# A 64-expert layer that sorts three of four batches instead of two, with its gathers and part of the next attention moved across the layer boundary

## The chip, the cores and the metric

The kernel runs on one core of a Trainium2 chip. The metric is device time in microseconds (us) of one execution, lower is better; times of several executions are given by their median.

## The reference, cut to what matters

The kernel is a decoder of four layers of three blocks on x of 4 batches x 512 tokens x 128 features, all in float32. The change touches the last block of layer 2 (64 experts), the first block of layer 3 (causal attention with 16 heads of 8 features), and, by a few lines, the gated delta rule (first block of layer 2).

```python
def _L2_ffn_ref(hidden_states, gate_w, w_gate, w_up, w_down):      # TOP_K = 8, 64 experts, D = 128, F = 96
    scores = softmax(x @ gate_w.T)
    topk_w, topk_ids = top_k(scores, TOP_K)
    topk_w = topk_w / (topk_w.sum(-1) + 1e-20)
    # every token through its 8 experts: silu(x @ w_gate[e].T) * (x @ w_up[e].T) @ w_down[e].T, weighted sum

def _L3_attn_ref(x, ...):                                          # H = 16, head size 8
    att = where(causal, q @ k.T / sqrt(8), -inf); att = softmax(att)
    y = (att @ v) @ Wo + bo
    return layernorm(y) * gamma + beta

x = x + _L2_ffn_ref(layernorm(x)); x = x + _L3_attn_ref(layernorm(x))
```

## The kernel before, in words

Activations x, y and a lie in SBUF with the 128 features on the partitions and the 4 x 512 tokens along the columns; a batch is 512 columns. Each engine has its own in-order instruction list, and semaphores join them. "Batch" below counts in the order of work where nothing else is said.

`layer8` (L1837) is the 64-expert block. It treats the four batches in two ways.

- Dense: batches 2 and 3 go through all 64 experts, with the weight zero where an expert was not chosen. The work is cut into 96 units (`unit`; two batches x J = 48 blocks of 128 rows of the 64 x 96 hidden features). A unit is three matmuls for the gate and three for the up part on values split in a high and a low half (`three`, L829), then silu on ScalarE (L2174), `scale` (L2324, times the routing weight) and `hidden` (L2330) on VectorE, and one float32 matmul `down` (L2049) that sums up in PSUM. The halves of the weights are made for each block by GpSimd for the first six blocks (L1939, L1941) and by ScalarE and VectorE after that (`split_high` L2169, `split_low` L2334), in three slots.
- Sorted: for batches 0 and 1 VectorE finds for each token its 8 experts and a row number in a list sorted by expert, padded to full tiles of 128 rows (`locate`, `situate`, `code`, `put`; indices are cast at L2305). GpSimd stores each token row eight times in DRAM with indirect DMAs (L1972, 64 of 128 rows each). TensorE then runs the tile stage: 127 tiles, two to a step (`PAIRS` = 64): transposed rows (L2055), gate and up (L2067), a transpose (L2075), down (L2082); VectorE evicts each pair (L2365), SP stores it, and `weigh` (L2293, L2294) sums one of the eight shares at every fourth step. GpSimd gathers the result rows with 64 indirect DMAs (L1979), VectorE multiplies and adds them (`mix`), and TensorE turns them back (`join`, L2088).

The order is routing, 48 dense units (`WIDE_SPLIT` = 24 blocks) with the indirect stores beside them, the tile stage, the other 48 dense units with the gathers and `mix` beside them, join. A store or gather waits for `down` as well, so that at most three are issued to two units.

`causal_attention` (L3072) follows. Its head centres and normalises all batches (L3152 to L3326) and projects q, k and v (L3171, L3173, L3178). A softmax needs each row's maximum first: a "read" (`look`, L3202, with a bfloat16 mask matmul L3198 where it lies on the diagonal) makes 1024 columns of scores, and VectorE takes their maxima (`most`, L3405). There are 20 reads to a batch. The head holds the 20 reads of batch 0 and 4 of batch 1. `turn_most` (L3211) and `shift` (L3414) put the maxima into the queries. Then come 16 units to a batch: `weigh` (L3221) makes transposed scores in two halves, ScalarE takes exponents (L3375), GpSimd's select zeroes what is above the diagonal (L3144), and `values` (L3236) sums up three units later (LAG = 3); four exponent buffers rotate (KEEP = 4). The reads of the next batch are spread over the units, at most two in one. Reads and weights share three pairs of PSUM banks in a ring: an item waits until the item three places ahead of it was consumed. The last part of each batch is the division by the row sums and the projection (`shift_sums` L3245, `project_out` L3249).

The delta rule's units also transpose their keys (L2631, phase KT) and copy them (L2902, phase K_COPY) for the update of the state.

## Time and profile before

| | us |
|---|---|
| median of three runs | 1896.92 (1888.32 to 1905.2) |
| the profiled execution's own time | 1892.54 |
| its span, first to last instruction | 1890.8 |
| expert block, from its first matmul to the attention's first | 1164.9 to 1527.4 |
| attention, head | 1527.4 to 1579.5 |
| attention, units | 1579.5 to 1767.5 |
| mean granted clock of TensorE, share of 2.4 GHz | 0.946 |

Over the whole span TensorE is busy for 89%, VectorE for 60%, ScalarE for 52% and GpSimd for 37%. Such shares are means over stages with different limits; the stages are read one by one below. In a timeline row the first number is the start in us from the span's start, the second the time covered, then engine, line, operation, output and input with their shapes, and in brackets how long the engine was idle before and what it waited for.

### The profile page before, as it was taken

Reading aid. Unit: us, or ns where it says so; the run is one execution under the profiler, and the core shown is the slowest. Engines: PE = TensorE matmul, PEld = TensorE weight load, DVE = VectorE, ACT = ScalarE, POOL = GpSimd, SP = SyncE. Lnnn points to the kernel's source line nnn. Section 1 sums busy time; section 2 is a strip of 40 time slices with the busy share of each in tenths; the row PEclk is TensorE's granted clock in tenths of the full one; section 3 lists DMA queues with packets and bytes.
Section 4 is the critical chain, followed back from the end, with each engine's and each line's share of the span. In section 5 each row is a group of like instructions: output and inputs, shape, how many; then the busy total and the mean of one; then the engine's idle time right before and its main releaser. Section 6 shows DMA issues by size and latency. Waiting matters only on the chain. (4 is left out here: it accounts for less than half of the span.)

```text
span 1890.8 us, 50187 instructions
## 1 busy us (share of the span) xinstructions
PE 1677.6 (89%) x19970; PEld 1202.2 (64%) x19970; DVE 1131.9 (60%) x2410; ACT 977.4 (52%) x2317; POOL 706.1 (37%) x947
## 2 busy tenths in 40 slices
PE   7883899775799999999999878899999999999885
PEld 4332899343457889989888753567996655454332
DVE  5534445559556777877776434676657866555334
ACT  4651444548586666666674435234553253445562
POOL 1103311305256777666775201473006621223101
PEclk9996999886699999999999989899999999999998
DMA  7401786000031000000000040523643200000100
GB/s 298 177 1 57 210 241 204 25 1 1 1 145 48 26 15 25 14 15 25 15 24 16 26 201 1 129 78 110 169 135 83 66 5 1 2 2 1 41 1 24
DMA packets 75929, 125.69 MB, mean 66 GB/s; under 512 B 10728, under 2 KB 55152, under 8 KB 74320
## 3 DMA queue, kind: packets, MB, share of 16 engines
q1 hardware_dynamic: 67696, 106.69, 17.5%
q0 software_dynamic: 6912, 15.61, 2.8%
q8 instruction: 165, 2.70, 0.6%
q14 instruction: 68, 0.56, 0.1%
q10 hardware_dynamic: 1088, 0.13, 0.0%
HBM read 83.73 MB, written 38.67 MB: 65 GB/s over the span
## 5 line engine op out<-in xcount | busy, mean ns | idle before, releaser
L2947 DVE SCALAR_TENSOR_TENSOR big<-bank,pack,big 128x256 f32<-128x256 f32 (+2 forms) x384 | 181.4, 474 | 40.6 <-ACT mask L2836 25.4
L2174 ACT ACTIVATE pack<-bank 128x512 f32<-128x512 f32 x96 | 57.5, 600 | 159.6 <-PE bank L834 93.8
L2643 PE MATMUL bank<-y,pack 128*128 128x262 f32 (+1 forms) x384 | 134.5, 435 | 5.5 <-DVE big L2947 5.1
L3375 ACT ACTIVATE pt<-bank 128x1024 f32<-128x1024 f32 (+3 forms) x128 | 84.2, 704 | 105.7 <-PE bank L3221 105.5
L3405 DVE TENSOR_REDUCE part<-bank 128x8 f32<-128x1024 f32 (+1 forms) x80 | 95.6, 1220 | 68.2 <-PE bank L3202 68.2
L2553 POOL TENSOR_TENSOR big<-big,mask 128x256 f32<-128x256 f32 (+1 forms) x128 | 93.7, 732 | 111.2 <-DVE big L2947 110.0
L2835 ACT ACTIVATE big<-bank,pack 128x256 f32<-128x256 f32 x192 | 91.1, 475 | 84.3 <-PE bank L2643 78.8
L1979 POOL DMA_INDIRECT pack<-results,where x64 | 67.0, 1047 | 151.2 <-PE bank L2049 137.6
L832 PE MATMUL bank<-yh,wl 128*128 128x512 f32 x192 | 113.3, 590 | 10.9 <-DVE a L2330 8.3
L2630 PEld LDWEIGHTS bank<-big 128*128 128x128 f32 x896 | 113.3, 193 | 7.1 <-issue 1.4
L2630 PE MATMUL bank<-big 128*128 128x128 f32 x896 | 116.2, 277 | 0.0
L3144 POOL TENSOR_SCALAR_AFFINE_SELECT pt<-pt 128x256 f32<-128x256 f32 x128 | 54.1, 427 | 156.8 <-ACT pt L3375 156.4
L1203 DVE SCALAR_TENSOR_TENSOR a<-bank,big,a 128x128 f32<-128x128 f32 x184 | 52.0, 344 | 82.4 <-ACT a L1115 72.3
L2049 PE MATMUL bank<-a,big 128*128 128x512 f32 x192 | 98.8, 598 | 0.8 <-DVE a L2330 0.8
L2324 DVE TENSOR_TENSOR pack<-pack 128x512 f32<-128x512 f32 x90 | 62.3, 693 | 50.0 <-ACT pack L2174 30.8
L3202 PE MATMUL bank<-big 32*128 32x128 f32 (+1 forms) x1024 | 84.1, 308 | 1.2 <-DVE part L3405 0.9
L1115 ACT ACTIVATE a<-bank,big 128x128 f32<-128x128 f32 x184 | 52.6, 368 | 59.0 <-PE bank L1012 51.9
L3202 PEld LDWEIGHTS bank<-big 32*128 32x128 f32 x1024 | 66.1, 186 | 24.0 <-issue 15.1
L3221 PE MATMUL bank<-big 32*128 32x128 f32 (+3 forms) x512 | 73.7, 477 | 5.2 <-DVE big L3414 2.5
L1972 POOL DMA_INDIRECT wide_sorted<-y,where x64 | 67.3, 1052 | 25.7 <-issue 17.2
L834 PE MATMUL bank<-yh,wh 128*128 128x512 f32 x192 | 76.3, 398 | 0.0
L833 PE MATMUL bank<-yl,wh 128*128 128x512 f32 x192 | 76.0, 396 | 0.0
(672 smaller groups left out, 4396.7 us busy)
## 6 DMA issues: line engine op xcount, KB each, us to landing
big<-in_experts SPq DMA_DIRECT2D x46, 516.0 KB
big<-in_big SPq DMA_DIRECT2D x1, 9216.0 KB, 25.9
gate<-big SPq DMA_DIRECT2D x32, 256.0 KB
z<-gate SPq DMA_DIRECT2D x16, 512.0 KB
pack<-routing SPq DMA_DIRECT2D x60, 128.0 KB
wide_sorted<-big SPq DMA_DIRECT2D x5, 1472.0 KB, 13.1
pack<-in_pack SPq DMA_DIRECT2D x1, 5910.5 KB, 21.5
pack<-wide_sorted SPq DMA_DIRECT2D x16, 256.0 KB, 3.2
```

The costliest lines, as they stand in the source:

```text
L832: nc.tensor.matmul(out, pl, dh[:, cur], start=start, stop=False)
L833: nc.tensor.matmul(out, ph, dl[:, cur], start=False, stop=False)
L834: return nc.tensor.matmul(out, ph, dh[:, cur], start=False, stop=stop)
L2049: nc.tensor.matmul(sums(n), down_block(n // 2), h(n), start=n < 2, stop=n >= N - 2).then_inc(s["down"], 1)
L2553: nc.gpsimd.tensor_tensor(d, d, tap_of(i)[:, :, c:], ALU.add).then_inc(s["whole"], 1)
L2630: mm4 = lambda out, gr, left_, right: [nc.tensor.matmul(out[:, sl(h % GH, P)], left_(h), right(h), start=True, stop=True) for h in hs(gr)][-1]
L2643: nc.tensor.matmul(haloed(i)[:, :, 3 - halo:], k.w["L2_attn_qkv_w"][:, sl(m, P)], tokens, start=True, stop=True).then_inc(s["raw"], 1)
L2835: nc.scalar.activation(dst3(i), conv_in(i, 0), ACT.Copy, scale=weight(i, 3))
L2947: ins = nc.vector.scalar_tensor_tensor(out=d, in0=conv_in(i, back), scalar=weight(i, 3 - back), in1=d, op0=ALU.mult, op1=ALU.add)
L3202: mm = nc.tensor.matmul(dst[:, gl * S + c * w:][:, 0:w], qj[b][rows, j * S + i * P:][:, 0:P], kd[b][rows, key:key + w], start=kind != 0, s ...
L3375: nc.scalar.activation(dst, src, ACT.Exp, scale=-1.0).then_inc(s["weights"], 1)
L3405: nc.vector.tensor_reduce(dst, src, AX.X, ALU.max).then_inc(s["most"], 1)
```

## The change

- Batches are taken in the order 2, 3, 0, 1. Only batch 2 stays dense: 48 units, one for each block, all before the tile stage; each block's weights are now split for one unit instead of two. `WIDE_POOLED` goes from 6 to 3.
- Batches 3, 0 and 1 are sorted: 96 indirect stores, 159 tiles in 80 pairs, vectors of the routing on 768 columns instead of 512. The stores no longer wait for `down`; they follow the indices directly.
- Between the dense units and the tile stage the first attention batch (batch 2) is centred and normalised, its q, k and v are projected, its own keys are made, and 6 of its 20 reads are taken.
- The gathers and sums move into the attention. GpSimd issues 32 of the 96 gathers at its start, ahead of the first select; the other 64 stand between the selects, one, two or four to a unit. ScalarE scales the gathered rows by their shares (`scale_rows`, 8 activations of 128x128 to a token tile, 96 in all), VectorE sums them with one reduction to a token tile (12 in all), and TensorE turns them back (`join`).
- The attention's head holds the other 14 reads of its first batch. Join, centring, variance, projections and own keys of batch b+1 stand in units 5 to 11 of batch b. Its 20 reads are packed in the last seven units (first batch: 2, 3, 3, 3, 3, 4, 2) or the last five (4, 4, 4, 5, 3).
- Constants are set by VectorE instead of GpSimd; the result rows' semaphores live across both blocks.
- In the delta rule the transposes and copies of the keys are left out in the last four units, whose state is not used again.

```diff
-WIDE_TILES = (2 * S * 8 + 64 * (P - 1)) // P
-WIDE_SPLIT, WIDE_POOLED, WIDE_MAP_AT = 24, 6, 13
-WIDE_MIX_AT = [2 * WIDE_SPLIT + 8 + 16 * i // 3 for i in range(8)]
+K8, WIDE_ORDER = 8, (2, 3, 0, 1)
+WIDE_ROWS = 3 * TB
+WIDE_TILES = (WIDE_ROWS * P * K8 + 64 * (P - 1)) // P
+WIDE_POOLED, WIDE_MAP_AT = 3, 13
...
+        late.qj = [big(24, 4)] + [big(4 * b, 4) for b in range(B - 1)]
+        late.kd = [big(28)] + [big(12 + b) for b in range(B - 1)]
...
+        late.kj = [big(30, 4), big(18, 4)]
...
+        layer8(nc, k, x, y, a, late)
+        causal_attention(nc, k, x, y, a, late)
...
-            for m in range(3, WIDE_POOLED):
-                split(m)
             pool.wait_ge(k.wide_cleared, 16 * -(-WIDE_TILES // SORTED))
-            pool.wait_ge(s["rows_ready"], 2)
+            pool.wait_ge(s["rows_ready"], 3)
             pool.wait_ge(s["placed"], 1)
-            for i in range(HALF):
+            for i in range(ROWS):
                 for c in range(K8):
-                    after(pool, s["down"], (i * K8 + c) * 2 // 3)
-                    nc.gpsimd.indirect_dma_start(out=rows_in, out_offset=bass.IndirectOffsetOnAxis(where[:, i * K8 + c:][:, 0:1], 0), in_=y[:, sl(i, P)], in_offset=None).then_inc(s["scattered"], 16)
-            for slot in range(4):
-                pool.wait_ge(s[f"stored_{slot}"], 16 * len(range(slot, PAIRS, 4)))
-            for i in range(HALF):
-                after(pool, s["mixed"], i - 1)
-                for c in range(K8):
-                    pool.wait_ge(s["down"], 2 * WIDE_SPLIT + 1 + (i * K8 + c) * 2 // 3)
-                    nc.gpsimd.indirect_dma_start(out=found[:, sl(i % 2 * K8 + c, P)], out_offset=None, in_=rows_out, in_offset=bass.IndirectOffsetOnAxis(where[:, i * K8 + c:][:, 0:1], 0)).then_inc(s[f"got_{i % 2}"], 16)
+                    nc.gpsimd.indirect_dma_start(out=rows_in, out_offset=bass.IndirectOffsetOnAxis(where[:, i * K8 + c:][:, 0:1], 0), in_=row_of(i), in_offset=None).then_inc(s["scattered"], 16)
...
-            for n in range(2 * WIDE_SPLIT + LAG):
-                if 0 < n < 2 * WIDE_SPLIT:
-                    unit(n)
-                if n >= LAG:
-                    down(n - LAG)
-                if n == WIDE_MAP_AT:
+            for m in range(J + LAG):
+                if 1 < m < J:
+                    unit(m)
+                if m >= LAG:
+                    down(m - LAG)
+                if m == WIDE_MAP_AT:
                     map_row()
+            pe.wait_ge(s["done"], 1)
+            nc.tensor.matmul(first_xc, k.w["centre"], x[:, sl(DENSE)], start=True, stop=True).then_inc(s["first_centred"], 1)
+            pe.wait_ge(s["first_squared"], 1)
+            nc.tensor.matmul(first_var, k.mean, first_sq, start=True, stop=True).then_inc(s["first_var"], 1)
+            pe.wait_ge(s["addressed"], 2)
+            pe.wait_ge(s["first_ready"], 1)
+            nc.tensor.matmul(q_bank, k.w["L3_attn_Wq"], late.y0, start=True, stop=True).then_inc(s["q_ps"], 1)
+            nc.tensor.matmul(k_bank, k.w["L3_attn_Wk"], late.y0, start=True, stop=True).then_inc(s["k_ps"], 1)
+            pe.wait_ge(s["consts"], 2)
+            for n in range(EARLY_LOOKS):
+                if n == 0:
+                    pe.wait_ge(s["k_out"], 1)
+                after(pe, s["most"], n - 2)
+                look_products(nc, k, late, 0, n, both(n)).then_inc(s["scores"], 1)
+                if n == 1:
+                    for t in range(TB):
+                        mm = nc.tensor.matmul(v_bank[:, sl(t, P)], late.y0[:, sl(t, P)], k.w["L3_attn_Wv"], start=True, stop=True)
+                    mm.then_inc(s["v_ps"], 1)
+            pe.wait_ge(s["v_out"], 1)
+            pe.wait_ge(s["most"], EARLY_LOOKS)
             pe.wait_ge(s["down_in"], 16)
-            pe.wait_ge(s["addressed"], 2)
             address(0)
             turn(0)
             for p in range(PAIRS + 2):
...
-            pe.wait_ge(s["tile_h"], PAIRS)
-            pe.wait_ge(s["tile_ht"], PAIRS)
-            for n in range(2 * WIDE_SPLIT, N + LAG):
-                if n < N:
-                    if n == 2 * WIDE_SPLIT + 1:
-                        pe.wait_ge(s["evicted"], PAIRS)
-                    unit(n)
-                down_of = n - LAG
-                if down_of >= 2 * WIDE_SPLIT:
-                    down(down_of)
-                if n == WIDE_MIX_AT[TB - 1] + 3:
-                    join(0)
-            join(1)
...
+            for m in range(J):
+                silu(m)
+            nc.scalar.preload_act_table_set(LN_EXP)
...
-    GROUPS, UNITS, KEEP, LAG, AHEAD = 4, 16, 4, 3, 4
...
-    per_unit = [(0, 1, 2, 2) * 3 + (0, 1, 0, 0)] + [(0, 2, 2, 2) + (0, 1, 2, 2) * 2 + (0, 2, 2, 0)] * 2
...
+def causal_attention(nc, k, x, y, a, late):
...
+    GROUPS, UNITS, KEEP, LAG = 4, 16, 4, 3
+    JOIN, QK, V, SHIFT = (5, 7, 7), (8, 10, 10), (9, 11, 11), (13, 13, 13, 13)
+    per_unit = [(0,) * 9 + (2, 3, 3, 3, 3, 4, 2)] + [(0,) * 11 + (4, 4, 4, 5, 3)] * 2
+    HEAD_GATHERS = 32
+    GATHERS = (1,) * 8 + (2,) * 6 + (1, 1) + (2, 2, 2, 2, 2, 1) + (1,) * 5 + (4,) * 5 + (2, 2, 1, 1)
...
+    def gathers_in(u):
+        done = HEAD_GATHERS + sum(GATHERS[:u])
+        return range(done, done + GATHERS[u]) if u < len(GATHERS) else range(0)
+
+    def mixes_in(b, m):
+        tile = m - (JOIN[b] - TB) if b + 1 < B else -1
+        return [b * TB + tile] if 0 <= tile < TB else []
+
+    next_at = lambda steps, b, m: b + 1 < B and m == steps[b]
+    ring = [("most", at) for at in range(left)]
     for u in range(B * UNITS):
+        b, m = divmod(u, UNITS)
         more = list(looks_in(u))
-        ring += [("weights", 2 * u)] + [("most", at) for at in more[:-1]] + [("weights", 2 * u + 1)] + [("most", at) for at in more[-1:]]
+        ring += [("weights", 2 * u)] + [("most", at) for at in more[:-1]]
+        if next_at(QK, b, m):
+            ring += [("k_out", b)]
+        ring += [("weights", 2 * u + 1)] + [("most", at) for at in more[-1:]]
...
+            def gather(n):
+                i, c = divmod(n, K8)
+                if c == 0:
+                    after(pool, s["mixed"], i - TB + 1)
+                nc.gpsimd.indirect_dma_start(out=found[:, sl(i % TB * K8 + c, P)], out_offset=None, in_=late.rows_out,
+                                             in_offset=bass.IndirectOffsetOnAxis(late.where[:, i * K8 + c:][:, 0:1], 0)).then_inc(s[f"got_{i % TB}"], 16)
+
+            pairs = -(-WIDE_TILES // 2)
+            for slot in range(4):
+                pool.wait_ge(late.s[f"stored_{slot}"], 16 * len(range(slot, pairs, 4)))
+            for n in range(HEAD_GATHERS):
+                gather(n)
             for u in range(B * UNITS):
+                b, m = divmod(u, UNITS)
                 for p in range(2):
                     pool.wait_ge(s["weights"], 2 * u + p + 1)
                     diagonal = pt[u % KEEP][:, sl(p, 2 * S)].rearrange("p (g q) -> p g q", g=2)[:, :, 0:P]
                     nc.gpsimd.affine_select(out=diagonal, in_=diagonal, pattern=[[0, 2], [1, P]], compare_op=ALU.is_ge, fill=0.0,
                                             base=0, channel_multiplier=-1).then_inc(s["kept"], 1)
-                if u % UNITS == 4 and 2 <= u // UNITS + 1 < B:
-                    spread(u // UNITS + 1)
+                if u == 0:
+                    pool.wait_ge(s["zeroed"], 2)
+                    spread(0)
+                for n in gathers_in(u):
+                    gather(n)
+                if b + 1 < B and m == min(V[b] + 3, UNITS - 1):
+                    spread(b + 1)

...
+            for at in range(left):
                 look(at)
-                if at in (1, 7, 13):
-                    project_qk(at // 6 + 1)
-                if at in (5, 11, 17):
-                    project_v(at // 6 + 1)
-            look(LOOKS)
             turn_most(0)
-            for at in range(LOOKS + 1, LOOKS + AHEAD):
-                look(at)
             for u in range(B * UNITS + LAG):
                 b, m = divmod(u, UNITS)
                 if u < B * UNITS:
                     if m % TB == 0:
                         pe.wait_ge(s["q_shifted"], u // TB + 1)
                     if m == 0:
+                        after(pe, s["k_own"], GROUPS * b)
                     weigh(u, 0)
                     for at in looks_in(u)[:-1]:
                         look(at)
+                    if next_at(QK, b, m):
+                        i = place["k_out", b]
+                        reuse(i)
+                        project_q_k(b + 1, both(i)[:, 0:S], both(i)[:, S:2 * S])
                     weigh(u, 1)
                     for at in looks_in(u)[-1:]:
                         look(at)
                 if 0 <= u - LAG < B * UNITS:
                     values(u - LAG)
-                if b and m == 4:
+                if 0 < b < B and m == 3:
                     shift_sums(2 * b - 1)
-                if b and m == 9:
+                if 0 < b < B and m == 5:
                     project_out(b - 1)
-                if b < B and m == 12:
+                if next_at(JOIN, b, m):
+                    join(b + 1)
+                if b + 1 < B and m == JOIN[b] + 1:
+                    centre(b + 1)
+                if b + 1 < B and m == JOIN[b] + 2:
+                    variance(b + 1)
+                if next_at(V, b, m):
+                    project_v(b + 1)
+                if b < B and m == SHIFT[b]:
                     shift_sums(2 * b)
                 if b + 1 < B and m == 15:
                     turn_most(b + 1)
...
+            def scale_rows(i):
+                act.wait_ge(s[f"got_{i % TB}"], 16 * K8 * (i // TB + 1))
+                for c in range(K8):
+                    row = found[:, sl(i % TB * K8 + c, P)]
+                    ins = nc.scalar.activation(row, row, ACT.Copy, scale=late.share[:, c * WIDE_ROWS + i:][:, 0:1])
+                ins.then_inc(s["rows_scaled"], 1)

...
-                if b and m == 5:
+                if b and m == 3:
                     invert_sums(2 * b - 1)
-                if m == 13:
+                for i in mixes_in(b, m):
+                    scale_rows(i)
+                if b + 1 < B and m == JOIN[b] + 1:
+                    square(b + 1)
+                if b + 1 < B and m == JOIN[b] + 2:
+                    invert(b + 1)
+                if next_at(QK, b, m):
+                    i = place["k_out", b]
+                    place_q_k(b + 1, both(i)[:, 0:S], both(i)[:, S:2 * S])
+                if next_at(V, b, m):
+                    own_keys(b + 1)
+                if m == SHIFT[b] + 1:
                     invert_sums(2 * b)
...
+            for n in range(2):
+                nc.vector.memset(vj[n][:, :], 0.0).then_inc(s["zeroed"], 1)
+                dve.wait_ge(s["zeroed"], 2 * n + 1)
+                nc.vector.memset(vj[n][:, :].rearrange("p (n e) -> p n e", e=64)[:, :, 16:24], 1.0)
+                nc.vector.memset(vj[n][:, :].rearrange("p (n e) -> p n e", e=64)[:, :, 56:64], 1.0).then_inc(s["zeroed"], 1)
+            for b in range(1, B):
+                nc.vector.memset(mx[b], 0.0).then_inc(s["zeroed"], 1)
+            dve.wait_ge(s["zeroed"], 4 + B - 1)
...
+                for i in mixes_in(b, m):
+                    mix(i)
+                if b and m == 4:
+                    divide(2 * b - 1)
                 if b and m == 6:
-                    divide(2 * b - 1)
-                if b and m == 10:
                     add_bias(b - 1)
-                if m == 14:
+                if next_at(JOIN, b, m):
+                    add(b + 1)
+                if b + 1 < B and m == JOIN[b] + 2:
+                    normed(b + 1)
+                if next_at(V, b, m):
+                    add_rows(b + 1)
+                if m == 15:
                     divide(2 * b)
                 if b + 1 < B and m == 15:
                     shift(b + 1)
-                if b in (1, 2) and m == 7:
-                    own_keys(b + 1)
...
-                elif phase == K_COPY:
+                elif phase == K_COPY and u // B < TB - 1:
```

## Rows read from the trace of the kernel before

**Rows 1.** PE, PEld, DVE, ACT, POOL busy (count), PEclk, DMA share, GB/s, by stage

```profile
1164.90:1307.10 142.20, 131.64 (x463) 86.23 (x464) 93.49 (x203) 45.95 (x85) 78.36 (x86) 0.92 0.34 95
1307.10:1407.40 100.30, 99.45 (x763) 94.88 (x762) 57.65 (x146) 57.73 (x160) 0.00 (x0) 1.00 0.53 149
1407.40:1527.40 120.00, 112.17 (x403) 73.49 (x402) 94.74 (x188) 35.47 (x71) 67.05 (x65) 1.00 0.27 69
1527.40:1579.50 52.10, 48.80 (x410) 30.46 (x412) 36.29 (x42) 27.39 (x41) 8.20 (x14) 0.97 0.00 1
1579.50:1733.90 154.40, 149.53 (x1532) 77.35 (x1528) 88.43 (x100) 69.70 (x106) 42.71 (x100) 1.00 0.01 1
1733.90:1767.50 33.60, 31.56 (x289) 12.01 (x289) 5.30 (x8) 22.05 (x36) 12.74 (x32) 1.00 0.01 1
```

**Rows 2.** Timeline of TensorE: two successive expert units of the dense batches

```profile
1279.62 1.02 PE L2049 MATMUL bank<-a,big 128*128 128x512 f32 x2
1281.86 1.02 PE L2049 MATMUL bank<-a,big 128*128 128x512 f32 x2
```

**Rows 3.** Timeline of TensorE in the tile stage: first matmuls of two pairs

```profile
1381.12 0.82 PE L2067 MATMUL bank<-big,pack 128*128 x4
1396.49 0.82 PE L2067 MATMUL bank<-big,pack 128*128 x4
```

**Rows 4.** Timeline of VectorE: the indices of the token rows are written

```profile
1196.21 0.20 DVE L2305 CAST where<-spot 128x64 int32<-128x64 f32 x1
```

**Rows 5.** Timeline of GpSimd: indirect stores of token rows; last line the SP queue

```profile
1204.74 1.09 POOL L1972 DMA_INDIRECT wide_sorted<-y,where  x1 [0.15 <-issue]
...
1246.72 1.07 POOL L1972 DMA_INDIRECT wide_sorted<-y,where  x1 [0.30 <-issue]
...
1256.25 0.96 POOL L1972 DMA_INDIRECT wide_sorted<-y,where  x1 [0.59 <-PE bank L2049]
1257.51 1.35 POOL L1972 DMA_INDIRECT wide_sorted<-y,where  x1 [0.30 <-issue]
...
1296.61 0.96 POOL L1972 DMA_INDIRECT wide_sorted<-y,where  x1 [0.59 <-PE bank L2049]
1298.86 1.48 SPq L1907 DMA_DIRECT2D pack<-wide_sorted  x3
```

**Rows 6.** Timeline of GpSimd: indirect loads of result rows

```profile
1416.15 0.95 POOL L1979 DMA_INDIRECT pack<-results,where  x1 [0.30 <-issue]
1417.41 0.95 POOL L1979 DMA_INDIRECT pack<-results,where  x1 [0.30 <-PE bank L2049]
```

**Rows 7.** Timeline of TensorE: first two reads of the attention; then two batch starts

```profile
1539.31 0.59 PE L3198 MATMUL bank<-later,ident_bf 128*128 128x512 bf16 x2
1540.92 0.60 PE L3198 MATMUL bank<-later,ident_bf 128*128 128x512 bf16 x2
...
1679.13 1.14 PE L3221 MATMUL bank<-big 32*128 32x512 f32 x8 [0.84 <-DVE big L3414]
...
1733.86 1.14 PE L3221 MATMUL bank<-big 32*128 32x512 f32 x8 [0.84 <-DVE big L3414]
```

**Rows 8.** Page, costliest groups: maxima of the reads; products with routing weights

```profile
L3405 DVE TENSOR_REDUCE part<-bank 128x8 f32<-128x1024 f32 (+1 forms) x80 | 95.6, 1220 | 68.2 <-PE bank L3202 68.2
L2324 DVE TENSOR_TENSOR pack<-pack 128x512 f32<-128x512 f32 x90 | 62.3, 693 | 50.0 <-ACT pack L2174 30.8
```

**Rows 9.** Timeline of ScalarE: a 128x128 activation; queries placed; own keys

```profile
1040.91 0.33 ACT L2930 ACTIVATE kt<-at 128x128 f32<-128x128 f32 x1
...
1535.47 2.79 ACT L3357 ACTIVATE big<-bank,qbias,pack 128x512 f32<-128x512 f32 x4
...
1541.22 2.91 ACT L3314 ACTIVATE big<-big,pack 128x512 f32<-128x512 f32 x4
```

**Rows 10.** Two lines by themselves: copies of transposed keys; splits of expert weights

```profile
L2902 ACT ACTIVATE kt<-bank x32: 597/598/617, 566.0 to 1064.1; 128x512 f32<-128x512 f32 x32
L2334 DVE TENSOR_TENSOR wl<-big,wh x42: 411/418/421, 1212.9 to 1512.4; 128x256 fp32r<-128x256 f32 x42
```

724 lines of the change are left out of this document (350 added, 374 removed).

## The prediction

> **What bounds the kernel now.** I read the busy time by stage first [rows 1]. In the tile stage, the second dense stretch and the attention's units TensorE is busy for 93 to 99% and no other engine for over 79%, so a change there is worth what it does to TensorE's list. The two places where TensorE isn't the limit alone are the routing with its first units (131.64 of 142.20 us busy, clock 0.92) and the attention's head (52.10 us, in which VectorE takes maxima of 1.22 us each [rows 8]). Then I took the periods from the timelines: a dense unit is 2.24 us (1281.86 - 1279.62) [rows 2]; ten pairs of tiles take 15.37 us, 1.54 a pair [rows 3]; the attention's batches are read from the first weights of the third and fourth, 1679.13 and 1733.86 [rows 7], so a batch with 20 reads in it takes 54.7 us, and the last, with none, 33.6 [rows 1]: 2.1 us a unit, and (54.7 - 33.6) / 20 = 1.06 us a read. The sum below is made on the profiled execution (1892.5 us; the median of the three runs is 4.4 us above it).
>
> **The expert block, part by part.**
> 1. Routing and dense units. 48 units of 2.24 us stay ahead of the tile stage, as before. The routing's vectors grow from 512 to 768 columns; most is hidden by units 0 to 2, and I charge 2 us (0 to 6). A block's split is now paid for one unit, not two; VectorE's window shows it busy 94.74 of 120.00 us [rows 1], and 24 more splits at 0.42 us [rows 10], 10 us, fit into its idle 25. Dense ends at 1307.1 + 2 = 1309.
> 2. The other 48 units go, with join and the change of stage: the window of 120.0 us [rows 1]. Of it only the change of stage, 1.4 us, stays.
> 3. Early work on the first attention batch. It is a chain through all engines, in which TensorE mostly waits. The old head took 1539.31 - 1527.4 = 11.9 us from its first matmul to its first read [rows 7]; the addition ahead of it is 0.9 (a VectorE pass over 512 columns as in [rows 8], and its wait), and six reads at 1.61 (1540.92 - 1539.31) with the last maximum are 10.9. TensorE is ready for tiles at about 1309 + 23 = 1332.
> 4. Indirect stores. Indices are written at 1196.2 [rows 4], and GpSimd began only at 1204.74, held by its own splits [rows 5]; now, with the longer vectors, I take 1199. Unthrottled they came 7 in 9.53 us, 1.36 apiece (1246.72 to 1256.25), where a plain step is 1.26 [rows 5, 6]. With a split in every unit I take 1.40: 79 are out when the dense part ends, and 17 at 1.27 follow, the last at 1331. The first load followed the last store by 2.25 us [rows 5]; with its landing I put 5.5 (estimate). Tiles start at 1337: stores, not the early reads, end last, by 5 us.
> 5. Tile stage. 100.3 us [rows 1] + 16 pairs x 1.54 = 24.6, and 2.4 for the eight sums of shares on 768 columns (0 to 5: VectorE has 42 us idle there). End 1337 + 127.3 = 1464.3; the attention starts at T = 1465.7, against 1527.4.
>
> **The attention.**
> 6. Head. 14 reads at 1.22 us [rows 8] and the turned maxima need some 21 us, and the first four units' weights follow by T + 26. But values(0) needs the first select, and 32 gathers stand ahead of it: 32 x 1.26 [rows 6] = 40.3, with the wait for the last stored tile and the select T + 43.5. Depth 4 lets nobody run on: TensorE stalls for about 17 us.
> 7. First batch after that: in units 4 to 8 a chain (sum, join, add, centre, square, variance, two activations, product, projections, queries placed) has one link per unit, and ScalarE carries it beside its exponents: a row set of eight scalings is 8 x 0.30 = 2.4 us (0.33 less the overlap of two), placing 2.79 for q and a quarter of it for k, own keys 2.91 [rows 9], exponents some 21 us a batch (22.05 in the last window, with 1.3 for row sums) [rows 1]. I take 18.5 us to the first read, T + 62. Seven units with 20 reads: 7 x 2.1 + 20 x 1.06 = 36, and 1 for the projection of v: T + 99. GpSimd pays 1.26 for each gather and about 0.9 for two selects, 2.2 or 3.4 us a unit, which units with 3 reads (5.3 us) cover.
> 8. Second batch. Units 0 to 10: ScalarE has 15.5 us of exponents (11 of 16 units, the wide ones first), 4 x 2.4 of scalings, 1.3 of row sums, then the same chain with waits; 38 us to the first read against 11 x 2.1 = 23 by TensorE's pace. Then 5 x 2.1 + 21.2 + 1 = 33: 71 us. The four gathers a unit, 4 x 1.26 + 0.9 = 5.9, just fit under four reads, 6.3. Third batch, with few gathers: 69. Fourth: 33.6. The tail is unchanged.
> 9. Delta rule. Eight copies of 0.60 us [rows 10] and their transposes go; TensorE has gaps there, so 2 us (0 to 5).
>
> **Sum.** The units of the last batch ended at 1767.5; after the change: 1465.7 + 99 + 71 + 69 + 33.6 = 1738.3, thus 29 us earlier; with the delta rule 31: 1892.5 - 31 = 1862. Put by parts: -120.0 + 1.4 (dense half), +29.9 (routing 2, early work and stores 27.9), +27.0 (tiles) and 272.6 - 240.1 = +32.5 for the attention with its head, -29 in all.
>
> A rule of the Trainium skill speaks against step 4. First the rows: one store in three takes 1.35 in place of 0.96 us beside the dense units [rows 5]. The Trainium skill (SBUF — State Buffer, "two separate sides") says that VectorE and GpSimd share a port pair under an exclusive lock, which a VectorE operation with two SBUF inputs takes too, and that indirect DMAs starve as GpSimd can't write descriptors. The trace agrees in kind, not in full size: three stores fitted into 4.49 us beside three such operations.
>
> **The rivals.**
> - A: TensorE bounds the attention too. For it: 149.53 of 154.40 us busy [rows 1], and the moved links are one to a unit. Then batch b+1's matmuls add about 5.6 us to 54.7: first batch 43.5 + 52, second and third 60.3 each, 216 us instead of 239. Against it: ScalarE's list in units 1 to 6. 1839 us.
> - B: the chain costs more. Each scaling waits for a gather, each gather for a sum four tiles back, each exponent for a select behind gathers. 8 us more in each of three batches: 1886, within 1% of before.
> - C, the slower side: GpSimd is the bound. Every VectorE operation with two SBUF inputs blocks a store fully: of two units (4.48 us) two products of 0.69 [rows 8] and two splits of 0.42 [rows 10] leave 2.26 us, less than two stores. At 2.5 us each 44 are out at 1309, the other 52 take 66 us, tiles start at 1380.5 (+43.5), and loads at 1.65 (1.35 + 0.30 [rows 5]) add 12.5 to the head: 1918. It makes the kernel slower than before once GpSimd costs 31 us more than in my sum. Against it: the 1.36 that was seen. This is what the rule above gives if taken in full.
> - D: the tile stage or the early work doesn't gain from the move (reads at half clock, the 17 us stall lets the clock fall: 1165 to 1195 had one at 0.92 over the window [rows 1]); 10 to 15 us more, 1875.
>
> **How the numbers follow.** My forecast (1850 to 1872) 0.38, A 0.24, B 0.14, C 0.12, D 0.12. The time is that of the likeliest, 1862 us. The range, 1832 to 1900, takes in A, B and D with the bounds of steps 1, 5 and 9, and leaves C and the far side of A out. About 1% is what a measurement of this kernel tells from no change; the limit is 1874. Faster by over 1%: forecast, A and half of D, 0.68. Within 1%: B and half of D, 0.20. Slower by over 1%: 0.12.
>
> **What would show it.** Dense unit period 2.24 with `h` waits absent; last store near 1331 and first tile near 1337, stores at 1.3 to 1.4 each; 80 pairs at 1.54; 32 gathers in 40 us at the attention's start and TensorE idle for 15 to 20 us before the first values, waiting for GpSimd; units 0 to 10 of batches two and three at 3 to 3.5 us each with TensorE waiting for ScalarE, units 11 to 15 at 6.3. I am wrong if stores take over 1.6 us (C), if units 0 to 10 run at 2.4 (A), or if the dense units slow down because VectorE has no slack left.

## The result, and the profile after

The changed kernel takes 2083.8 us (median of four runs, 2066.7 to 2095.2), the kernel before 1895.9 in the same measurement: a ratio of 1.098 (95% interval 1.089 to 1.108). The forecast was 1862. The profiled execution took 2095.2 us, with a span of 2093.3 and a mean granted clock of 0.869, against 0.946 before.

That number holds for the chip of this measurement at that time. A session is a set of kernels run one after another on one chip; five followed the measurement. Sessions 3 and 4 gave the unaltered changed kernel 1942.7 us (a1: ratio 1.032, 1.026 to 1.037) and 1937.1 (a3: 1.027, 1.021 to 1.033), session 5 again 2073.9 (a4, one execution, beside 1893.2). The change is slower everywhere, for two reasons, each of which the runs show without the other. I call them the stall, which only some sessions show, and the attention's packed reads, which all show.

Where the time stands, from the timelines (first select: GpSimd's first work on attention weights):

| | forecast | a1 | measured change |
|---|---|---|---|
| dense units end | 1309 | 1312.0 | 1422.6 |
| first tile's first matmul | 1337 | 1341.1 | 1451.7 |
| last indirect store begins | 1331 | 1326.9 | 1328.7 |
| first to last tile pair's silu (before: 96.3) | 123.3 us | 127.3 us | 127.3 us |
| first select | 1509.2 | 1517.5 | 1648.1 |
| first batch, its first select to the next batch's | 55.5 | 76.5 | 81.8 |
| second batch | 71 | 94.1 | 105.8 |
| third batch | 69 | 90.8 | 101.3 |
| profiled execution | 1862 | 1937.1 | 2095.2 |

Of the 233 us between forecast and measurement, 138.9 lie ahead of the first select and 93.4 in three batches. In a1 it is 8.3 and 65.9 of 75. Executions also differ ahead of all this: the first down projection starts at 1203.8 in the measured change and at 1196.1 in a1, so 7.7 us of what stands between these two columns is older than the stretch below.

First the stretch that [rows 1] showed at 98% TensorE. Four windows of the changed kernel (columns: PE, PEld, DVE, ACT, POOL busy, granted clock, DMA share, GB/s):

```profile
1220.00:1240.00 20.00, 8.60 (x27) 5.17 (x27) 4.98 (x10) 1.80 (x4) 15.13 (x17) 0.84 0.55 151
1240.00:1260.00 20.00, 4.34 (x9) 2.19 (x9) 1.72 (x3) 0.90 (x2) 15.28 (x16) 0.59 0.15 52
1300.00:1320.00 20.00, 5.00 (x12) 2.73 (x12) 1.78 (x3) 0.90 (x2) 15.13 (x17) 0.59 0.15 50
1360.00:1380.00 20.00, 20.00 (x74) 13.55 (x72) 18.04 (x32) 8.12 (x18) 0.00 (x0) 1.00 0.15 40
```

From 1240 to 1328 only GpSimd is busy, with 16 indirect stores in 20 us; TensorE, VectorE and ScalarE are busy for 21, 8 and 5 us of 100, and the DMA engines are idle for 85%. The last store begins at 1328.7; TensorE is back at full pace from some 1344 on, 15 us later, and the fourth window has it at 20 of 20. One unit in that stretch, TensorE first, then ScalarE, VectorE and GpSimd:

```profile
1258.95 0.80 PE L833 MATMUL bank<-yh,wl 128*128 128x512 f32 x1 [15.66 <-issue]
1259.54 0.63 PE L834 MATMUL bank<-yl,wh 128*128 128x512 f32 x1
1259.97 0.63 PE L835 MATMUL bank<-yh,wh 128*128 128x512 f32 x1
1260.40 0.63 PE L833 MATMUL bank<-yh,wl 128*128 128x512 f32 x1
...
1261.68 1.91 PE L2099 MATMUL bank<-a,big 128*128 128x512 f32 x2
1281.35 0.80 PE L833 MATMUL bank<-yh,wl 128*128 128x512 f32 x1 [17.77 <-issue]
```
```profile
1271.87 0.60 ACT L2218 ACTIVATE pack<-bank 128x512 f32<-128x512 f32 x1 [21.50 <-remote]
```
```profile
1272.50 0.69 DVE L2382 TENSOR_TENSOR pack<-pack 128x512 f32<-128x512 f32 x1 [13.61 <-issue]
1280.27 0.69 DVE L2388 TENSOR_TENSOR a<-bank,pack 128x512 f32<-128x512 f32 x1 [7.07 <-issue]
1280.88 0.42 DVE L2392 TENSOR_TENSOR wl<-big,wh 128x256 fp32r<-128x256 f32 x1
```
```profile
1260.16 0.96 POOL L2027 DMA_INDIRECT wide_sorted<-y,where  x1 [0.30 <-issue]
1261.43 0.96 POOL L2027 DMA_INDIRECT wide_sorted<-y,where  x1 [0.31 <-issue]
1262.69 0.96 POOL L2027 DMA_INDIRECT wide_sorted<-y,where  x1 [0.30 <-issue]
```

Read the releasers with care. "Issue" and "remote" mean that the profile knows no cause. VectorE's scale follows the silu at once (1272.47 to 1272.50) and TensorE follows VectorE's split at once (1281.30 to 1281.35), so neither these engines nor signals in general are late. The silu waits for the gate product, whose third matmul is recorded at 1259.97, and comes 11.3 us after that one's end; the `h` product waits for the up product (1261.25) and comes 18.4 us later. What TensorE hands on is late. The period is 22.40 us for eight matmul records, 2.8 us each on average, though the records themselves start 0.4 us apart. From silu to `h` it is 8.40 us, and three matmuls, those of the up product, lie between: 2.8 us each again. The attention's head shows such steps in the records themselves: while the 32 indirect reads run, after the first 16, TensorE gets out one small matmul at a time.

```profile
1616.65 0.36 PE L1855 MATMUL bank<-big 32*128 32x128 f32 x1 [2.43 <-issue]
1620.15 0.37 PE L1855 MATMUL bank<-big 32*128 32x128 f32 x1 [3.13 <-issue]
1622.25 0.36 PE L1855 MATMUL bank<-big 32*128 32x128 f32 x1 [1.74 <-issue]
1625.05 0.37 PE L1855 MATMUL bank<-big 32*128 32x128 f32 x1 [2.43 <-issue]
```

These are 128 columns wide, those of the expert block 512, and both come to 2.8 us apiece, so the time seems to go by matmuls and not by columns. The steps of these starts are 3.50, 2.10 and 2.80 us, all multiples of 0.70; the runs don't say of what.

### The profile page after: what moved, and what is told of

Read it like the earlier page. It is cut to its first block and busy times, and to the rows that moved or that the text cites. A ratio compares the mean times of both kernels' runs of the same rounds, so it can differ in the third digit from the quotient of the medians.

```text
span 2093.3 us, 49773 instructions
## 1 busy us (share of the span) xinstructions
PE 1702.1 (81%) x19738; PEld 1208.0 (58%) x19758; DVE 1096.8 (52%) x2309; ACT 997.1 (48%) x2413; POOL 741.9 (35%) x994
## 5 line engine op out<-in xcount | busy, mean ns | idle before, releaser
L2999 DVE SCALAR_TENSOR_TENSOR big<-bank,pack,big 128x256 f32<-128x256 f32 (+2 forms) x384 | 181.4, 474 | 40.5 <-ACT mask L2886 25.3
L3191 POOL DMA_INDIRECT pack<-results,where x96 | 91.3, 951 | 287.8 <-SPq L51 258.5
L833 PE MATMUL bank<-yh,wl 128*128 128x512 f32 x96 | 58.6, 611 | 97.9 <-issue 80.5
L1855 PE MATMUL bank<-big 32*128 32x128 f32 (+1 forms) x1024 | 114.6, 408 | 22.0 <-issue 19.5
L1855 PEld LDWEIGHTS bank<-big 32*128 32x128 f32 x1024 | 92.7, 263 | 58.6 <-issue 48.9
L2218 ACT ACTIVATE pack<-bank 128x512 f32<-128x512 f32 x48 | 28.7, 600 | 180.6 <-remote 90.8
L2027 POOL DMA_INDIRECT wide_sorted<-y,where x96 | 93.1, 969 | 59.2 <-DVE where L2362 30.3
L3278 PE MATMUL bank<-big 32*128 32x128 f32 (+3 forms) x512 | 95.7, 603 | 10.7 <-ACT pt L3424 5.8
L833 PEld LDWEIGHTS bank<-yh,wl 128*128 128x128 f32 x96 | 20.4, 213 | 119.0 <-issue 95.1
L1116 ACT ACTIVATE a<-bank,big 128x128 f32<-128x128 f32 x184 | 52.6, 368 | 59.1 <-PE bank L1013 52.6
L2382 DVE TENSOR_TENSOR pack<-pack 128x512 f32<-128x512 f32 x45 | 31.3, 696 | 86.4 <-issue 57.6
L2691 PEld LDWEIGHTS bank<-y,pack 128*128 128x128 f32 x384 | 61.3, 195 | 22.6 <-DVE big L2999 8.1
L3278 PEld LDWEIGHTS bank<-big 32*128 32x128 f32 x512 | 38.4, 226 | 59.8 <-issue 33.3
```

What stands on the lines that cost most here:

```text
L833: nc.tensor.matmul(out, pl, dh[:, cur], start=start, stop=False)
L1855: mm = nc.tensor.matmul(dst[:, gl * S + c * w:][:, 0:w], late.qj[b][rows, j * S + i * P:][:, 0:P], late.kd[b][rows, key:key + w], start=ki ...
L2027: nc.gpsimd.indirect_dma_start(out=rows_in, out_offset=bass.IndirectOffsetOnAxis(where[:, i * K8 + c:][:, 0:1], 0), in_=row_of(i), in_offs ...
L2691: nc.tensor.matmul(haloed(i)[:, :, 3 - halo:], k.w["L2_attn_qkv_w"][:, sl(m, P)], tokens, start=True, stop=True).then_inc(s["raw"], 1)
L2999: ins = nc.vector.scalar_tensor_tensor(out=d, in0=conv_in(i, back), scalar=weight(i, 3 - back), in1=d, op0=ALU.mult, op1=ALU.add)
L3191: nc.gpsimd.indirect_dma_start(out=found[:, sl(i % TB * K8 + c, P)], out_offset=None, in_=late.rows_out, in_offset=bass.IndirectOffsetOnAx ...
```

## Experiments on the stall

**Session 1: how many are under way, and does the kernel before have it?** e1 gives the stores four semaphores in turn, so that a store is issued only when the one four back has landed; e2 does so for the reads, e3 for both.

```diff
+                    n = i * K8 + c
+                    after(pool, s[f"open_{n % 4}"], 16 * (n // 4))
                     nc.gpsimd.indirect_dma_start(out=rows_in, ...
-                        in_=row_of(i), ...).then_inc(s["scattered"], 16)
+                        in_=row_of(i), ...).then_inc(s[f"open_{n % 4}"], 16)
```

> The changed kernel with its 96 indirect stores on four semaphores in turn, so that at most four of them are under way. Theory Q (a backlog: back-to-back indirect DMAs are handed over faster than they are carried out, and once some 16 are queued TensorE's signals reach ScalarE and VectorE late, 11 and 7 us a unit in 1240 to 1340): the units keep to 2.3 to 2.8 us, the dense stage ends near 1330 to 1350 instead of 1420, the total is 1995 to 2025 us. Theory P (any indirect DMA beside the dense units costs this, whatever is queued): the stretch 1240 to 1340 stays at 3.6 to 5.0 us of TensorE work in 20 and the total within 20 us of 2084.

> The changed kernel with the 96 indirect reads of the attention on four semaphores in turn, at most four under way; the stores run free as they did. Theory Q: the stretch of single matmuls each 2.4 to 3.1 us (1606 to 1631) goes and the first selects come some 20 us earlier if the reads keep their pitch of 1.25, total 2050 to 2070 us; the dense stage is as slow as before. Theory P: no change at all in that stretch, total 2075 to 2100.

> Both limits together. Theory Q: the two gains add, 1965 to 2005 us. Theory P: within 20 us of 2084.

Measured: 2066.3, 2076.5 and 2077.9 us. Theory Q fell. GpSimd's waits in e1, 1215 to 1345 (line waited for: us in total, times, longest):

```profile
POOL wide_sorted L2030 <- issue: 26.6, 87, 0.4
POOL wide_sorted L2030 <- DMA wide_sorted<-y,where: 11.2, 3, 8.3
```

The limit held GpSimd three times; all other stores had landed within four pitches (5.1 us). So there is no pile of unfinished transfers, yet from 1260 to 1280 TensorE worked 4.64 of 20 us (3.59 in the measured change). The limit on the reads in e2 did as little: the first select came 60.0 us after the first read, against 59.9.

e4 is the kernel before with the wait of its stores for `down` taken out:

```diff
-                    after(pool, s["down"], (i * K8 + c) * 2 // 3)
```

> The kernel before with one line taken out: its 64 indirect stores no longer wait for the down projections (two counts for three stores), so they are issued back to back at 1.27 us, 1204 to 1286. Theory Q: TensorE's units go from 2.24 to over 10 us each from some 1225 until the last store, its dense stretch ends 45 to 60 us later, total 1935 to 1960 us. Rival (the stall belongs to something else that the change put into this stretch, such as reading y of three batches or the 96-row table loads): the kernel before is not slower, 1890 to 1905 us.

Measured: 1958.7 us beside 1906.7. Two windows:

```profile
1240.00:1260.00 20.00, 4.97 (x8) 2.32 (x8) 1.72 (x3) 0.60 (x1) 15.12 (x17) 0.56 0.14 49
1260.00:1280.00 20.00, 1.62 (x3) 0.83 (x3) 0.74 (x1) 0.90 (x2) 15.24 (x16) 0.50 0.15 52
```

The same stall, without anything else of the change. In session 1 that one wait was what spared the kernel before, and the change had dropped it.

**Session 2: the rate.** e5 puts a GpSimd memset of 128x256 behind every store, e6 the old wait back.

```diff
+                    after(pool, s["down"], min((i * K8 + c) * 2 // 3, J))      # e6
                     nc.gpsimd.indirect_dma_start(out=rows_in, ...)
+                    nc.gpsimd.memset(pause[:, :], 0.0).then_inc(s["paced"], 1)  # e5
+                    pool.wait_ge(s["paced"], i * K8 + c + 1)                    # e5
```

> The changed kernel with one GpSimd memset of 128x256 behind every indirect store, so that a store comes every 1.6 to 1.8 us in place of 1.27, with no tie to TensorE. Theory R (the rate of issue: GpSimd issuing indirect DMAs back to back at 1.27 us is what slows TensorE's instructions; the kernel before stayed under that with 1.48 on average): the dense units keep 2.3 to 2.6 us to the end, done by 1330; the last store is at 1207 + 96 x 1.7 = 1370, tiles start at about 1375 in place of 1451, total 2000 to 2020 us. Rival (time since the first store, or the stores as such): TensorE still falls to some 4 us in 20 from 1240 on, and the total is 2080 or more.

> The changed kernel with the old rule put back: store n waits for 2n/3 down projections (three stores to two units), at most all 48. Theory R: 72 stores go out beside the dense units at 1.49 apiece, these keep 2.24 and end near 1320; the last 24 run free beside the early attention work, 30 us, which gets slow in its last 10 us; tiles start near 1355, total 1985 to 2010 us. Rival: no better than 2065 us.

Measured: 1975.6 and 1984.7 us beside a kernel before of 1886.4; dense units at 2.25 us to the end (last down projection at 1313.4 and 1311.2). Taken alone this confirms the rate, and it would have been wrong to stop here: in the same session e7 and e8 (below), whose expert block is that of the changed kernel, had no stall either. The session did not show it at all. So I ran the unaltered kernel again.

> The changed kernel, nothing altered. In two runs (e7, e8) whose expert block is this kernel's line for line, TensorE kept 2.24 us a unit beside stores at 1.27 to 1.39, and the tiles started at 1343 and 1348 in place of 1453. Theory B (two ways to run: with TensorE at pace, VectorE's work stretches one store in five to 1.39 us and the pair stays under the limit; once TensorE is late, VectorE is idle, the stores run at 1.265 and TensorE stays late; a small thing at the start decides): executions of this kernel fall into two groups, near 1970 to 1985 and near 2070 to 2095, or all into the quick one. Rival (what decides is in the program, its layout in memory, which the attention's code shifts): all at 2065 to 2100 again.

> The kernel before without the wait of its stores, as e4. Theory B: it is slow only in some executions: near 1890 or near 1955. If it is in the program: 1950 to 1965 each time.

Measured in session 3: a1 1942.7 us (1937.1 to 1956.1, four runs), a2 1885.5 beside 1884.8 (ratio 1.000, 0.998 to 1.002). Nothing in the program differed. Where a session ran a kernel more than once, its times agree within 2% (2066.7 to 2095.2, 1937.1 to 1956.1), so it is neither the program nor a chance of each execution. Session 4 was calm too, session 5 was not.

> The changed kernel unaltered, on whatever chip this call gets. Theory C (the stall beside free indirect DMAs belongs to the chip: five kernels with it in the first call and in the measurement of the change, none in the two later calls): near 1943 with 96 stores at 1.27 to 1.39 and TensorE at 2.24 a unit, or near 2084, and then e16 beside it must show that spacing helps.

> e5 again (a memset of 128x256 behind each indirect store). On a chip that shows the stall, theory R (rate of issue): dense units at 2.24 to 2.6, 60 to 80 us under the unaltered kernel beside it. On a chip without it: 10 to 30 us over the unaltered kernel, as the last store comes 25 us later.

> The changed kernel unaltered, on whatever chip this call gets: near 1940 on one without the stall, near 2084 on one with it.

> A memset of 128x64 behind each indirect store, for a pitch of some 1.5 us, near the 1.48 of the kernel before. On a chip with the stall, theory R (rate): dense units at 2.24, 70 to 90 us under a4. Without the stall: 5 to 20 us over a4, since the last store comes later.

> e5 a third time (128x256 behind each store, 1.65 us). On a chip with the stall, theory R: dense units at 2.24 to 2.6 and 60 to 80 us under a4; if the stall stays, rate is not the cause. Without the stall: some 40 us over a4, as e16 was over a3.

Here e16 and e19 are e5 again, and e17 is e5 with a memset of 128x64. Measured: a3 1937.1 and e16 1981.6 us in the calm session 4, where spacing costs 45 us (49 between the profiled executions: the first select comes 26 us later, and the first two batches take 14 and 9 us more, at a lower mean clock). In session 5: a4 2073.9, e17 1993.1, e19 2011.5. Session 5 is the test, as the stall is there in a4 and gone in e17 and e19. The window 1240 to 1260 of a4, then of e17, and e17's unspaced reads in the head:

```profile
1240.00:1260.00 20.00, 4.64 (x8) 2.49 (x8) 1.55 (x3) 0.90 (x2) 15.12 (x17) 0.50 0.18 62
```
```profile
1240.00:1260.00 20.00, 20.00 (x72) 13.38 (x72) 17.07 (x31) 7.88 (x18) 16.32 (x27) 1.00 0.27 83
1500.00:1520.00 20.00, 7.46 (x33) 4.53 (x31) 2.64 (x3) 0.00 (x0) 15.13 (x17) 0.50 0.20 54
```

A memset of 0.17 us behind each store brought TensorE from 4.64 to 20.00 of 20 us, and the last down projection from 1415.3 to 1316.2; the reads behind it, not spaced, stalled in the same run (first select 59.7 us after the first read). These are single executions, but the 81 and 62 us that e17 and e19 gained on a4 are far beyond the 2% above. Mean pitch of the stores from 1240 to 1300, first to last start over their count less one: 1.27 us in the measured change and in a4 (47 stores), 1.38 in a1 and a3 (44), 1.52 in e17 (40), 1.69 in e19 (36), 1.50 in the kernel before (38).

The 1.38 of a1 is the same program as the 1.27. GpSimd in a1:

```profile
1263.16 0.96 POOL L2027 DMA_INDIRECT wide_sorted<-y,where  x1 [0.30 <-issue]
1264.43 0.96 POOL L2027 DMA_INDIRECT wide_sorted<-y,where  x1 [0.31 <-issue]
1265.69 0.96 POOL L2027 DMA_INDIRECT wide_sorted<-y,where  x1 [0.30 <-issue]
1266.96 1.24 POOL L2027 DMA_INDIRECT wide_sorted<-y,where  x1 [0.30 <-issue]
```

With VectorE at work (49.05 of 60 us in a1, 1240 to 1300) some stores are stretched; with VectorE waiting (7.64 of 100 us in the measured change, 1240 to 1340) one of 47 is (1.22 us, 1240 to 1300), against eleven of 44 in a1. So a late TensorE makes the stores faster, which is the wrong way round for recovery. Whether this feedback helps to decide which way a session goes was not tried. The Trainium skill (SBUF — State Buffer, "two separate sides") has TensorE never waiting on anyone at its SBUF ports, and, where VectorE holds the pair that it shares with GpSimd, GpSimd as the one that is held. The runs agree in kind with the second half (the stretched stores) and show the first to be no shield here: TensorE loses nine tenths of its pace (22.40 us a unit for 2.24) while GpSimd issues. Whether any port is the path isn't shown.

## Experiments on the attention

> The changed kernel with 8 indirect reads ahead of the first select in place of 32; the other 24 go six to a unit behind the selects of units 0 to 3. The first select comes 25 to 35 us earlier than T + 66 and TensorE does not fall to single matmuls before 1630; total 2050 to 2065 us. If the late head is the look products at half clock (14 x 2.97 = 42 us) and not the reads, the first select gains only 10 us and the total is 2070 to 2080.

e8 (session 2, calm) issues 8 reads ahead of the first select in place of 32, and six in each of units 0 to 3 (`HEAD_GATHERS = 8`, `GATHERS = (6,) * 4 + (2,) * 4 + ...`). From the first read to the first select it took 25.3 us, a1 took 39.8: 14.5 gained. But the first batch took 119.0 us in place of 76.5, since its chain waits for these reads (ScalarE 22.6 us in all, in a1 not at all). Total 1995.6, 58 us over a1's profiled execution. Of that, 28 us are this exchange (42.5 lost for 14.5 gained), so the 32 reads ahead of the selects are better placed than they look, in a calm session. Another 26 are in the second and third batches (110.3 and 100.8 us, against 94.1 and 90.8), whose reads are placed as in a1 and ran longer at half clock.

The batches: units 0 to 10 of the second take 45.6 us in a1, units 11 to 15 with their 20 reads 48.5. In the third it is 43.7 and 47.1, and there the last indirect read is at 1697, 9 us in. So the indirect reads are not the cause of the long units 11 to 15. Four windows of a1 around the start of the second batch's reads, then TensorE:

```profile
1626.00:1630.00 4.00, 3.46 (x23) 1.07 (x22) 0.00 (x0) 3.86 (x7) 2.67 (x5) 1.00 0.06 16
1638.00:1642.00 4.00, 2.62 (x18) 1.82 (x18) 0.00 (x0) 1.50 (x3) 0.41 (x1) 0.55 0.08 20
1642.00:1646.00 4.00, 4.00 (x24) 2.14 (x22) 1.81 (x2) 0.00 (x0) 0.00 (x0) 0.50 0.00 0
1658.00:1662.00 4.00, 4.00 (x48) 2.21 (x46) 3.33 (x5) 1.02 (x1) 0.72 (x2) 1.00 0.02 4
```
```profile
1639.38 1.01 PE L1851 MATMUL bank<-later,ident_bf 128*128 128x512 bf16 x2 [3.27 <-ACT big L3386]
1640.32 2.08 PE L1855 MATMUL bank<-big 32*128 32x128 f32 x16
1642.33 1.03 PE L1851 MATMUL bank<-later,ident_bf 128*128 128x512 bf16 x2
1643.29 2.08 PE L1855 MATMUL bank<-big 32*128 32x128 f32 x16
1645.30 1.03 PE L1851 MATMUL bank<-later,ident_bf 128*128 128x512 bf16 x2
```

A read takes 1645.30 - 1642.33 = 2.97 us, against 1.61 in [rows 7]: the granted clock is 0.50 (1.2 GHz) though TensorE is busy all the time. It fell in the wait of 3.27 us for ScalarE to place q and k, just ahead of the reads, and was back at 1.00 some 17 us later (0.50 from 1638.4 to 1655.4). The return isn't always so quick. In the measured change the same wait (3.46 us) was followed by 34 us of half clock, here without its first 1.7 us, and then the stretch behind it:

```profile
1778.00:1810.30 32.30, 31.64 (x202) 20.15 (x202) 12.24 (x13) 6.06 (x8) 9.21 (x12) 0.50 0.07 18
1810.40:1830.80 20.40, 15.83 (x156) 8.89 (x154) 13.66 (x14) 3.89 (x7) 12.23 (x17) 1.00 0.12 30
```

Four kernels fill waits by making the weight products several times into the same bank, which adds work for TensorE and nothing else:

```diff
-                for gl in range(2):
+                for gl in [0, 1] * (3 if b + 1 < B and m < 10 else 1):                       # e7
+                for gl in [0, 1] * ((4, 5, 6, 10)[c] if b + 1 < B and 2 < m < 11 else 1):     # e10
+                # e13: as e10 up to m == QK[b], and at m == QK[b] + 1, p == 0: 14 times (first batch 8)
+                # e14: as e13, but only the three units up to QK[b], and QK[b] + 1
```

> The changed kernel with each pair of weight products of units 0 to 9 of the first three batches made three times into the same bank (same result). It adds 400 matmuls and is there to keep TensorE busy in the waits of the chain. Theory H (half of the attention's loss is the clock: a read takes 2.97 us where TensorE was idle before it, 1.61 in the kernel before): the granted clock is 0.9 or more in the second and third batch, the reads there take 1.6 to 1.9 us, these batches come down from 106 and 101 us to 80 to 90, total 2030 to 2055 us. Rival (the chain of waits sets the batch, the clock only follows): batches over 100 us and total 2080 to 2120.

> The changed kernel with the stores waiting for down projections as in e6 (no stall in either case) and the weight products of units 3 to 10 of the first three batches made 4, 5, 6 or 10 times, by their width. e6 was 1985. Theory H (clock): in e7 the clock was back at 1.0 only from 1675 on, after 18 us of reads at 0.5; with more padding it stays up through the chain, units 11 to 15 fall from 49 to 56 us to 35 to 40, total 1925 to 1950. If padding only moves the wait: 1965 or more.

> e10 with one gap more closed: the first pair of weight products behind the projection of q and k (unit 11, in the first batch unit 9) is made 14 (8) times, 3 us beside ScalarE's placing of q and k. In e10 the clock was 1.0 through the chain and fell to 0.5 in that one wait of 3.3 us (1682 to 1686), for 30 us of reads. Theory H: the reads now run at 1.0, 1.6 to 1.75 us each, units 11 to 15 take 38 to 42 us in place of 48 to 56, total 25 to 40 us under e10's 2005 (to its own kernel before: 1.045 or less). If the clock falls anyway or the reads stay at 2.97: within 10 us of e10.

> The same, but the padding only in the last three units before the reads (units 8 to 10, in the first batch 6 to 8) and beside the placing; the rest of the chain as in the changed kernel. Theory H: the padding costs the chain some 5 us a batch instead of 15, the clock has time to come back, and the total is 10 to 25 us under e13. If three units are too short, the reads run at 0.5 and the total is over e13's.

(The lines on e13 and e14 tell their changes in words.) Measured: 1966.7, 2004.9, 1965.6, 1976.6 us. e7's session had no stall, so its distance to 2084 says nothing; its second batch took 103.0 us, the rival's figure, as the clock still fell ahead of the reads. e10 and e14 missed their forecasts of the total too, and e13 alone met its own. In the second and third batches e10 and e13 differ only in the padding over ScalarE's placing. Windows of e10 around the second batch's first read, then of e13:

```profile
1676.00:1680.00 4.00, 4.00 (x24) 2.27 (x22) 0.31 (x1) 0.60 (x1) 0.41 (x1) 1.00 0.00 0
1684.00:1688.00 4.00, 2.27 (x14) 1.47 (x16) 0.00 (x0) 1.85 (x4) 0.41 (x1) 0.66 0.07 20
1692.00:1696.00 4.00, 4.00 (x28) 2.33 (x28) 2.40 (x3) 1.20 (x3) 0.60 (x2) 0.50 0.00 0
```
```profile
1668.00:1672.00 4.00, 4.00 (x45) 2.62 (x46) 2.09 (x2) 0.00 (x0) 0.38 (x1) 1.00 0.00 0
1680.00:1684.00 4.00, 4.00 (x45) 2.05 (x44) 3.32 (x4) 1.02 (x1) 1.35 (x2) 1.00 0.00 0
```
```profile
1669.39 0.61 PE L1851 MATMUL bank<-later,ident_bf 128*128 128x512 bf16 x2
1669.92 1.16 PE L1855 MATMUL bank<-big 32*128 32x128 f32 x16
1671.02 0.60 PE L1851 MATMUL bank<-later,ident_bf 128*128 128x512 bf16 x2
```

In e10 the clock was 1.00 all through the chain and fell in that one wait; in e13 it stayed, and a read takes 1671.02 - 1669.39 = 1.63 us. Units 11 to 15: 56.0 and 46.0 us in e10 (second, third batch), 48.5 and 47.1 in a1, 41.1 and 41.3 in e13. Theory H is shown for the reads: against e13's 41.1 and 41.3, half clock costs a1 7.4 and 5.8 us in these batches, and a single wait sets it off. As an improvement it fails, because the padding lengthens units 0 to 10 from 45.6 to 60.4 us, and e13 is 28 us behind a3 in its own session (6 of them from its later tile stage: the stores wait for `down` there). Its 39 us against e10 are no gain over the unpadded kernel. In e14 the clock was 0.50 from 1650 to 1658 and 1.00 from 1662, ahead of the second batch's reads at 1682, and units 11 to 15 took 41.1 us: with three padded units the clock was up in time. They are also as dear as eight (units 0 to 10 took 59.1 us), and the three batches are 5 us shorter than e13's in all; that the total is 11 us over e13's comes from what lies ahead, as its first tiles came 14.5 us later, 11.3 of which were there at the first down projection.

## Why the prediction was wrong, point by point

- **What bounds (steps 1 to 3).** Right where there is no stall: dense units 2.24, end 1312 (1309). The early work took 29 us to the first tiles, not 23, at a clock of 0.59 (1320 to 1340 in a1), and so the tiles waited for it and not for the stores: first tile's matmul at 1341.1, where I had 1337. Step 9, the delta rule, can't be seen: the first down projection comes at 1196.1 in a1 and 1195.0 in the kernel before, with the longer routing between.
- **Step 4, stores.** Pitch beside dense units 1.38 in a1 (1.40), last store 1326.9 (1331). In the measured run 1.27: nothing held them. The failed step is what is missing: I priced the stores on GpSimd's own list and gave the dropped waits for `down`, of stores and of reads, no price at all. What they had held off cost 103 us here (end of the dense units 1422.6 against 1312.0 in a1, less the 7.7 us by which the run was late at the first down projection) and 20.1 in the head (59.9 against 39.8 us from first read to first select). I had seen that stores ran 7 in 9.53 us for a short while; no row of the kernel before shows them back to back for longer than the first 17, and its own window after these is the one hint that was there, as TensorE worked 15.20 of 20 us in it. The first three rows are the kernel before, with its wait; the last is a2, without the wait but in a calm session, where that dip is absent:

```profile
1200.00:1220.00 20.00, 20.00 (x73) 13.43 (x72) 13.18 (x23) 5.41 (x10) 13.14 (x15) 1.00 0.80 191
1220.00:1240.00 20.00, 15.20 (x51) 9.48 (x49) 9.93 (x18) 5.30 (x11) 13.61 (x15) 0.91 0.33 112
1240.00:1260.00 20.00, 20.00 (x74) 13.51 (x72) 13.80 (x24) 6.61 (x13) 14.55 (x14) 1.00 0.26 86
...
1220.00:1240.00 20.00, 20.00 (x73) 12.99 (x72) 14.28 (x26) 6.31 (x13) 15.43 (x16) 1.00 0.40 130
```

- **Step 5, tiles.** Close: from the first to the last silu 127.3 us, against 96.3 in the kernel before, 31.0 more where I had 27.0.
- **Step 6, head.** Right in a1: first select 39.8 us after the first read (40.3 forecast for 32 reads). With the late tiles it stands at 1517.5, 8.3 us behind. In the measured run the stall made it 59.9.
- **Steps 7 and 8, the failed terms in every session.** "2.1 us a unit and 1.06 us a read" came from batches in which the reads were spread. A unit without reads took 2.1 us; beside reads of 1.61 us it took only (54.7 - 20 x 1.61) / 16 = 1.41, so there a read partly fills time that a unit alone leaves free (whose gap that is was not measured). Packed four or five to a unit the reads find no such time: 20 x 1.61 + 5 x 1.41 + 1 = 40 us, 41 in e13, and I had 33. Half clock adds 5.8 to 7.4. The chain of units 0 to 10 adds 7.6 in the second batch (45.6 against 38) and 7.7 in the third (43.7 against the 36 that a batch of 69 leaves). In sum +23.1 and +21.8 in a1. The first batch is 21.0 over: its first read came 28.0 us after the first select where I had 18.5, and the rest took 48.5 us, not 37; that part wasn't taken apart further. In the measured run the second and third batches took 11.7 and 10.5 us more still, 10.5 and 7.5 of them in units 11 to 15, where the mean granted clock was 0.67 and 0.69 against 0.84 and 0.83 in a1: the 34 us of half clock in place of 17. The calm session 2 had this as well (e6 63.3 and 54.6 us for these units), so it doesn't belong to the stall.
- **Rivals.** C, the slower side, had the right engine and the wrong mechanism: VectorE's lock was to slow the stores to 2.5 us each, and they ran at 1.27, faster than forecast. It was said to be a rule of the Trainium skill (SBUF — State Buffer, "two separate sides") taken in full, which goes beyond that section: it ties the starving of descriptors to VectorE's two-port modes, and of operations with two SBUF inputs it says that they take the lock only against a GpSimd operation that reads SBUF. B had the right size for the chain (8 us a batch, measured 7.6 and 7.7), but not the reads' cost. D named the half clock but for 10 to 15 us in all. A is refuted (60.3 us a batch, measured 94.1 and 90.8). The forecast of slower by over 1% had 0.12.
- **Open.** Why the clock comes back after 17 us in one run and after 34 in another. Why a matmul takes 2.8 us while GpSimd issues without a gap: a slow supply of TensorE's instructions isn't seen, as the one instruction transfer on queue q8 from 1225 to 1335 took 0.96 us (in a1 four, of 0.88 to 1.39). And what makes one session show the stall and another not: the chip with number 5 was calm in session 3, and one with that number showed it in session 5.

## What to carry to other kernels

A wait that paces a queue can be doing work that its engine's own list doesn't show; before dropping one, look for what runs unpaced elsewhere in the trace, and if nothing does for as long, give the unknown its own rival on the slow side. A marginal cost read from spread-out work (1.06 us a read) is not the cost of the same work packed (1.61): take the engine's own duration for it. And run the unaltered kernel again beside each set of experiments, as two of these would have "confirmed" a cure in a session that wasn't ill.

## What the runs showed of the hardware that was not expected

Indirect DMAs issued by GpSimd every 1.27 us cut TensorE to about one matmul in 2.8 us, of 128 or 512 columns alike, in three of six sessions (the measurement, 1 and 5), from some 20 us after the first of them (stores from 1207.7, `h` late from 1226.9; reads from 1588.2, single matmuls from 1608.2). At a pitch of 1.52 us (e17) there was no effect in such a session, and in calm ones none at 1.25 either (32 reads in a row in a1). The clock went from 1.00 to 0.50 in a TensorE wait of 3.3 us and came back only after 17 us (a1) and 34 us (e10), in which TensorE was busy from the end of the wait on (16.0 of 16.0 us in a1, 32.8 of 32.8 in e10); in e6 it stayed at 0.50 for 55 us, the last 47.4 of them without a gap on TensorE.
